# Output product and own embedding of the chosen rows once per two groups, another order of the start, and new lists of steps in a ViT block on one core

## The reference

```python
pooled = x.reshape(64, 12, 14, 16, 14, 16).sum(axis=(3, 5))          # sums of 16x16 patches
h = jnp.einsum('bcij,ce->bije', pooled, channel_weights)              # (64, 196, 192)
y = _layernorm(h)
qkv = y @ Wqkv_w + Wqkv_b                                             # 12 heads of 16
attn = softmax(q @ k^T * 0.25 + causal_mask)                          # mask: -10000 above the diagonal
attn_output = ctx @ out_w + out_b
selection = softmax((y @ sel_w + sel_b) / temperature)[..., 1:]
_, idx = jax.lax.top_k(selection[..., 0], 14)
y = y.at[idx].add((attn_output * selection)[idx])                     # chosen rows alone
h = h + y
h = h + gelu(_layernorm(h) @ in_weight.T + in_bias) @ out_weight      # hidden width 768
```

## Time and profile before

| | |
|---|---|
| median of 3 runs | 708.93 us (699.64 to 709.5) |
| profiled execution | 706.07 us |
| its span, first to last instruction | 704.4 us |
| PE busy | 576.7 us, 82% |
| DVE busy | 522.0 us, 74% |
| ACT busy / POOL busy | 335.0 us / 251.9 us |
| granted PE clock, mean | 0.942 of full speed |

### The profile page before, as it was taken

The page is one execution under the profiler, slowest core; times in us unless marked ns, Lnnn a source line. Parts: engine busy times, 40 slices in busy tenths (PEclk is TensorE's granted clock), DMA queues, the critical chain, the costliest instruction groups (busy, mean ns, idle before and its releaser), DMA issues.

```text
span 704.4 us, 12381 instructions
## 1 busy us (share of the span) xinstructions
PE 576.7 (82%) x3860; PEld 475.4 (67%) x3860; DVE 522.0 (74%) x1103; ACT 335.0 (48%) x826; POOL 251.9 (36%) x484
## 2 busy tenths in 40 slices
PE   0228048899997999889998979799988999899995
PEld 0117027686976787768876777678767887788784
DVE  1767977797979888888887867988888888753411
ACT  0000044565554656554655445465645465547541
POOL 1220433444344525352535323452535253304001
PEclk9998557999999999999998989999999999999998
DMA  9996895989797979887997669797997795001001
GB/s 326 348 363 193 302 350 174 342 276 343 240 336 268 300 253 345 285 302 222 331 302 275 209 232 320 247 309 246 333 302 289 227 331 140 13 10 41 26 9 40
DMA packets 34892, 172.54 MB, mean 245 GB/s; under 512 B 3688, under 2 KB 19240, under 8 KB 22538
## 3 DMA queue, kind: packets, MB, share of 16 engines
q1 hardware_dynamic: 20224, 143.14, 56.0%
q0 software_dynamic: 6912, 11.70, 9.6%
q10 hardware_dynamic: 7690, 16.89, 6.7%
HBM read 158.99 MB, written 12.73 MB: 244 GB/s over the span
## 4 chain that ended last, share of the span: by engine, by line
PE 44%; DVE 18%; issue 16%; POOL 8%; DMA 6%; ACT 5%; POOLq 1%; DVEq 0%; SPq 0%; ACTq 0%
PE psO L637 15%; DMA X<-in_x 6%; PE psS L588 6%; DVE R L942 5%; PE psS L597 4%; PE psF L625 4%; PE psS L576 3%; PE psA L542 2%; DVE mx L1056 2%; PE psS L561 2%; ACT ET L754 2%; POOL b_ln L391 1%; DVE a_ln L952 1%; DVE b_ln L954 1%; DVE y_ln L956 1%
## 5 line engine op out<-in xcount | busy, mean ns | idle before, releaser
L942 DVE TENSOR_REDUCE R<-X 128x42 f32<-128x2688 f32 (+1 forms) x112 | 260.5, 2339 | 15.6 <-POOL X L352 8.5
L637 PE MATMUL psO<-W,act 128*112 128x192 f32 x1344 | 261.8, 339 | 11.9 <-ACT obuf L779 4.0
L637 PEld LDWEIGHTS psO<-W,act 128*112 128x112 f32 x1344 | 223.3, 183 | 18.2 <-issue 7.3
L772 ACT ACTIVATE act<-psF 128x392 f32<-128x392 f32 x192 | 95.3, 496 | 123.1 <-PE psF L625 121.2
L352 POOL TENSOR_TENSOR X<-X 128x1344 f32<-128x1344 f32 x32 | 96.9, 3027 | 21.3 <-DMA X<-in_x 21.1
L361 POOL TENSOR_TENSOR Pt<-Praw 48x196 f32<-48x196 f32 x16 | 8.6, 538 | 191.3 <-DMA Praw<-patch_sums 191.3
L625 PE MATMUL psF<-Stk,M1S 104*128 104x392 bf16 x192 | 66.1, 344 | 5.5 <-ACT act L772 4.8
L1067 DVE TENSOR_TENSOR G<-psS,K 64x336 f32<-64x336 f32 x32 | 16.0, 501 | 44.7 <-PE psS L588 44.2
L588 PE MATMUL psS<-ET,F 98*64 98x336 f32 x128 | 39.6, 452 | 10.4 <-ACT ET L754 10.4
L750 ACT ACTIVATE Sm<-Sm,rinv 112x196 f32<-112x196 f32 x96 | 35.3, 445 | 18.9 <-DVE rinv L1062 18.7
L745 ACT ACTIVATE Sm<-psS,nm 112x196 f32<-112x196 f32 x96 | 39.2, 427 | 7.3 <-DVE nm L1059 7.2
(11 more groups left out here) (197 smaller groups left out, 954.1 us busy)
## 6 DMA issues: line engine op xcount, KB each, us to landing
X<-in_x SPq DMA_DIRECT2D x96, 1344.0 KB, 8.6
X<-in_x SPq DMA_DIRECT2D x16, 672.0 KB, 4.6
X<-in_x POOLq DMA_DIRECT2D x16, 672.0 KB, 12.8
out<-obuf ACTq DMA_DIRECT2D x16, 588.0 KB, 8.7
patch_sums<-R ACTq DMA_DIRECT2D x16, 147.0 KB, 7.9
Praw<-patch_sums ACTq DMA_DIRECT2D x16, 147.0 KB, 6.5
W1T<-in_w1t ACTq DMA_DIRECT2D x1, 576.0 KB
W<-in_w ACTq DMA_DIRECT2D x1, 576.0 KB
```

What stands on the lines that cost most here:

```text
L637: pe.matmul(to, act_sb[u % 2][:, m, i * OT:(i + 1) * OT], W2[:, m, :], start=(m == 0), stop=False)
L772: act.activation(act_sb[u % 2][:, n // 2, (n % 2) * (GT // 2):(n % 2 + 1) * (GT // 2)], psF[:, 0:GT // 2], ACT.Gelu).then_inc(act_F1.sem, 1)
L942: dve.tensor_reduce(R[:, r, t * TQ * N:(t + 1) * TQ * N].rearrange("p (q j) -> p q j", q=TQ), v, AX.XY, ALU.add).then_inc(dve_L, 1)
```

## The change

1. **Chosen rows once per pair.** ZY, G2, dsm, dsel, res and h1 hold both groups of a pair (56 rows, 8 unused, 56 rows). `rs` and `at` are issued for the second group alone and give 120 rows; `rs` goes to psC. G2, ZY and dsel get a memset at the start.
2. **The start.** `prepare` is gone. `first_group` on DVE sums the seven tiles of group 0 between the weight steps and puts the head copies, A4, B2 and the bf16 parts of RS behind the last sum; tiles 0 and 1 of group 1 are summed there too. ACT issues the small selection weights first, W1T once X0 has landed, the attention weights once X2 has, W2 once X5 has.
3. **The lists** of all four engines are new. DVE's `L` steps and `log` move back, PE's `zt` moves ahead and `sl` behind `at:1`, POOL's `c:s` moves behind `H:0`, ACT's exps move from the start of a period to the end of the one before.

```diff
-        ZY = sb("ZY", [FR, SLOTS])
+        ZY = sb("ZY", [FR, 2, ODD])
-        G2 = sb("G2", [128, HP, SLOTS])
-        dsm, dsel = sb("dsm", [SLOTS, GB]), sb("dsel", [SLOTS, 1])
+        G2 = sb("G2", [128, HP, 2, ODD])
+        dsm, dsel = sb("dsm", [PROWS, GB]), sb("dsel", [PROWS, 1])
...
-            plan = ("X:3:1 P:s:2 c:s:5 H:5:1 A:var2:2 K:v:2 K:d1:2 K:d2:2 H:0:0").split()
+            plan = ("P:s:2 H:5:1 A:var2:2 K:v:2 K:d1:2 K:d2:2 H:0:0 c:s:5 X:3:0").split()
...
                     if exists(g - 1):
-                        pe.wait_ge(dve_S.sem, dve_S.at(g - 1, "h1"))
+                        pe.wait_ge(dve_S.sem, dve_S.at(g - 1, "g1"))
+                    if u % 2 == 0 and exists(g - 2):
+                        pe.wait_ge(dve_Q.sem, dve_Q.at(q - 1, "h1"))
...
-                    pe.wait_ge(dve_G.sem, dve_G.at(g, "ix"))
-                    mm = pe.matmul(psS[0:SLOTS, 0, D:2 * D], ZY[:, :], BW[:, :], start=True, stop=True)
...
+            def step_rs(g, q):
+
+                pe.wait_ge(dve_G.sem, dve_G.at(g, "zy"))
+                if exists(g - 2):
+                    pe.wait_ge(dve_C.sem, dve_C.at(q - 1, "os1"))
+                pe.matmul(psC[0:PROWS, 0:D], ZY[:, :, :].rearrange("p e s -> p (e s)")[:, 0:PROWS], BW[:, :],
+                          start=True, stop=True).then_inc(pe_Q.sem, 1)
...
-                mm = pe.matmul(psS[0:SLOTS, 0, 0:D], G2[:, j, :], B2[:, j, :], start=(j == 0), stop=(j == HP - 1))
+                mm = pe.matmul(psS[0:PROWS, 0, 0:D], G2[:, j, :, :].rearrange("p e s -> p (e s)")[:, 0:PROWS], B2[:, j, :],
+                               start=(j == 0), stop=(j == HP - 1))
...
                     elif stage == "at":
-                        step_at(g, 2 * int(step))
-                        step_at(g, 2 * int(step) + 1)
+                        if u % 2:
+                            step_at(g, 2 * int(step))
+                            step_at(g, 2 * int(step) + 1)
...
+                act.dma_start(Wsel[0:DH, :, :], selw.rearrange("(k d) n -> d k n", k=2)).then_inc(w_sel, 16)
...
+                act.wait_ge(x_in[0], loaded(0))
                 act.dma_start(W1T[0:DH, :, :], w1t.rearrange("(k d) n -> d k n", k=2)).then_inc(w_ffn, 16)
...
+                act.wait_ge(x_in[2], loaded(0))
                 act.dma_start(Wqkv[0:DH, :, :], wqkv.rearrange("(k d) n -> d k n", k=2)).then_inc(w_att, 16)
...
+                act.wait_ge(x_in[5], loaded(0))
+                act.dma_start(W2[:, :, :], w2.rearrange("(h p) e -> p h e", h=HT)).then_inc(w_out, 16)
...
-            plan = ("S:e0:2 S:e1:2 S:e2:2 S:e3:2 S:e4:2 S:e5:2 O:0:2 S:n:2 O:1:2 A:fm:1 K:H:1 S:t:2 K:M:1 O:2:2 "
-                    "K:L:1 A:e:1 O:3:2 R:st:0 K:k1:1 K:k2:1 f:0:1 f:1:1 f:2:1 f:3:1 O:4:2 R:ld:0 f:4:1 f:5:1 f:6:1 "
-                    "O:5:2 f:7:1 G:rs:1 C:XH:2 f:8:1 C:ga:2 f:9:1 f:10:1 O:6:2 C:gb:2 f:11:1").split()
+            plan = ("K:H:1 S:t:2 K:M:1 A:fm:1 K:L:1 O:3:2 G:rs:2 R:st:0 K:k1:1 A:e:1 K:k2:1 f:0:1 f:1:1 f:2:1 f:3:1 "
+                    "R:ld:0 f:4:1 O:4:2 f:5:1 f:6:1 O:5:2 f:7:1 f:8:1 C:XH:2 f:9:1 f:10:1 C:ga:2 O:6:2 f:11:1 C:gb:2 "
+                    "S:e0:1 S:e1:1 S:e2:1 S:e3:1 S:e4:1 S:e5:1 O:0:1 S:n:1 O:1:1 O:2:1").split()
...
+            def first_group():
+
+                sum_tile(0, 0, 0)
+                weights_first()
+                sum_tile(0, 0, 1)
+                weights_moments()
+                sum_tile(0, 0, 2)
+                weights_tokens()
+                sum_tile(0, 0, 3)
+                sum_tile(0, 0, 4)
+                weights_ffn()
+                sum_tile(0, 0, 5)
+                weights_parts("M")
+                sum_tile(0, 0, 6)
+                for m in range(3):
+                    weights_heads(m)
+                weights_attention("a4")
+                sum_tile(1, 1, 0)
+                weights_attention("b2")
+                sum_tile(1, 1, 1)
+                weights_parts("R")
+
-            plan = ("C:os:4 S:g:3 A:sel:2 L:0:0 A:top:2 S:at:3 A:slots:2 G:ga:2 C:xh:3 L:1:0 G:u:2 L:2:0 S:sc:2 "
-                    "A:var:1 L:3:0 S:ri:2 L:4:0 A:log:1 L:5:0 L:6:0").split()
+            plan = ("A:log:2 S:g:3 A:sel:2 C:os:4 A:top:2 S:at:3 A:slots:2 G:ga:2 C:xh:3 L:0:0 G:u:2 L:1:0 S:sc:2 "
+                    "A:var:1 L:2:0 S:ri:2 L:3:0 L:4:0 L:5:0 L:6:0").split()
```

More of the change, by code:

```diff
@@ L248, in program @@
         dve_W = Steps(sem("dve_weights"), "wr0 ws0 xh0 h10 as0 ini idb ms ms2 wcs rf mr mr2 wcr bw0 bw1 wt ws cf cf2 raw sd sd2 s1 tp tz tmm tmd tmb m1 "
-                      + " ".join(f"{n}{t}" for t in "MR" for n in splits.split()) + " q k v a4 b2 ob")
+                      + " ".join(f"{n}M" for n in splits.split()) + " q k v a4 b2 ob " + " ".join(f"{n}R" for n in splits.split()))
         block = ctx.enter_context(nc.Block())
@@ L478, in weights @@
                 mm.then_inc(pe_W.sem, 1)
+                pe.wait_ge(w_ffn, NW_FFN * 16)
                 for n in range(2):
@@ L561, in step_G, with step_S @@
                         mm = pe.matmul(psS[0:ZR, 1 + h // HP, (h % HP) * SLOTS:(h % HP + 1) * SLOTS], A4[:, h, :],
[L562 to L566 removed]
+                                       ZY[0:ZR, r, 0:SLOTS], start=True, stop=True)
                 mm.then_inc(pe_G.sem, 1)
[L569 removed]
+            def step_S(g, u, name, q):
                 r = u % 2
@@ L631, in step_F2 @@
                 if m == 0:
+                    if i == 0 and isinstance(g, int) and g == 0:
+                        pe.wait_ge(w_out, 16)
+                        pe.wait_ge(dve_W.sem, dve_W.at(0, "alR"))
                     if i == 0:
@@ L653, in body @@
                         continue
-                    if stage == "C":
+                    if stage == "C" and step == "rs":
+                        if u % 2:
+                            step_rs(g, pair_of(i, k, lag))
+                    elif stage == "C":
                         if u % 2:
@@ L733, in step_R, with step_G @@
                     act.dma_start(Praw[:, r, :], sums_in[bass.ds(g, 1)].rearrange("o p q -> (o p) q")).then_inc(sums_back[r], 16)
-            def step_G(g, u, name):
-                act.wait_ge(pe_G.sem, pe_G.at(g, "rs"))
-                act.activation(res[:, :], psS[0:SLOTS, 0, D:2 * D], ACT.Copy).then_inc(act_G.sem, 1)
+            def step_G(q):
+                act.wait_ge(pe_Q.sem, pe_Q.at(q, "rs"))
+                act.activation(res[:, :], psC[0:PROWS, 0:D], ACT.Copy).then_inc(act_Q.sem, 1)
             def step_S(g, u, name):
@@ L799, in body @@
                         step_F2(g, u, int(step))
+                    elif stage == "G":
+                        if u % 2:
+                            step_G(pair_of(i, k, lag))
                     elif stage == "f":
@@ L1126, in body @@
                     if stage == "L":
-                        if isinstance(i, int) and k == 0:
-                            prepare(int(step))
-                        sum_tile(g, u % 2, int(step))
+                        if not (isinstance(g, int) and (g, int(step)) < (1, 2)):
+                            sum_tile(g, u % 2, int(step))
                     elif stage == "S":
-                        stage_S(g, u, step, pair_of(i, k, lag))
+                        if step != "at" or u % 2:
+                            stage_S(g, u, step, pair_of(i, k, lag))
                     elif stage == "C":
@@ L1136, in body @@
                         {"A": stage_A, "G": stage_G}[stage](g, u, step)
-                if isinstance(i, int) and k == 0:
-                    weights_attention("a4")
-                    weights_attention("b2")
             weights_zeroed()
+            first_group()
             periods(nc.vector, body, 8, 2)
 NW_CW = 1 + PAIRS + 2 * GB + 2
-NW_FFN = 5
-NW_ATT = 5
+NW_SEL = 3
+NW_FFN = 2
+NW_ATT = 4
 def kernel(x, L0_tok_channel_weights, L0_attn_Wqkv_w, L0_attn_Wqkv_b, L0_attn_sel_w, L0_attn_sel_b, L0_attn_out_w,
```

83 lines of the change are left out of this document (36 added, 47 removed), and 3 rows, old and new, of the table plan.

## The result

| | before | changed |
|---|---|---|
| median, first comparison | 707.89 us (699.64 to 709.5) | 719.48 us (711.81 to 733.63) |
| ratio to before | 1 | 1.0172, 95% interval 1.0117 to 1.0227 |
| again, on another chip | 705.96 us | 716.6 us, ratio 1.0166 (1.0129 to 1.0203) |

The changed kernel is 1.7% slower: +12 us where -14 were forecast. Here and in what follows the medians hold every execution, while ratios and intervals leave out the slow ones (over 1.5% above the fastest of their kernel), so where the two differ the ratio counts. Its profile is shown from the execution of the second comparison, 715.07 us with a span of 713.3; the first comparison's profile fell on an execution that took 14 us more than the median.

What follows compares the result with a forecast made beforehand. PE bounds heavy stretches; in light ones POOL's fold holds DVE's nm and PE waits. Terms -8.8 + 2 - 1.5 - 1.2 - 4.5 = -14.0 from 706.07 give 692 us, 8-in-10 range 682 to 706.

Steps and rivals of the forecast that it cites:

- -8.8 - 0.5 - 1.0: Light stretches: 1.7 us less in each of five, 0.3 in a sixth; 0.5 and 1.0 less in the first and last.
- So the work leaves mostly where PE is not the bound: Chosen rows once per pair: at (2.4 us) leaves light stretches, rs (some 0.46 us) leaves heavy ones.
- With a fallen clock in about half of them (1.5 us for twelve records in rows 2) I take 35.4 us.: Light stretch: 34.7 us laid out, 35.4 taken with the clock's fall; bounds 33.3 and 37.
- The fold still meets `nm`: Light stretch: fold runs from 18.9 to 22.0 us behind S:g, nm ready at 20.1, freed 2.8 us earlier than before.
- rival A: Light stretches: the fold ends before nm, the clock holds, 33.6 us, -3.5 each, 683 us in all; chance 0.17.
- Heavy stretches, +0.3 each: Heavy stretches: rs and scores' wait saved, later sl leaves PE dry; +0.3 us each, +2 over seven, bounds -0.5 and +0.9.
- the loop's turn, -1.2: ACT's loop turn moves between O:2 and K:H, ahead of the exps before: -1.2 us, bounds -3 and +1.
- the forecast 42: Sign in the new profile: a window of about 42 us where ACT's loop turns.
- The start, -4.5 us: Start: DVE's sums end at 57.7 instead of 65.74, var starts about 74 instead of 77.83; -4.5 us, bounds -6 and -2.
- no fold runs beside `prod`: Start, DVE: prod runs without a fold beside it, which saves 1.2 us of its 1.48.
- Rival C: Heavy stretches: xh meets tile 5's fold, up to 3.0 us in each of seven, 21 us added, 713 us; chance 0.1.
- Rival D: Chosen rows once per pair: the pairing does nothing, as PE work leaves where PE waits; within the forecast, no separate chance.

Runs made afterwards that it cites:

- lists and start, no pairing: The kernel before with the new lists and the new start, chosen rows still made for every group by itself: 693.98 us, ratio 0.9877.
- POOL's list alone: The kernel before with one line of POOL's list changed, two indirect DMAs moved behind the fold of tile 0: 690.27 us, in more rounds 690.61 us (0.9776).
- changed with filler: The changed kernel with at's six matmuls issued in light stretches too, their result unread, 2.4 us more PE work each: 695.16 us, ratio 0.9887.
- changed with late six: The changed kernel with the same six unread matmuls in light stretches, but behind the scores, right ahead of rs: 714.99 us, ratio 1.0051.
- lists alone: The kernel before with the new lists, old start, rs and at issued for every group: 698.03 us, ratio 0.9898.
- two unread matmuls: The changed kernel with two of at's six matmuls issued unread in light stretches, in the gap ahead of sl: 707.85 us, ratio 1.0035.

## Why the prediction was wrong

Span by parts, in us; light and heavy are the sums of eight and seven windows of the kernel's profile:

| | to first `S:g` | light | heavy | behind the last `S:g` | span |
|---|---|---|---|---|---|
| before | 129.37 | 285.6 | 262.5 | 26.96 | 704.4 |
| changed | 130.11 | 289.8 | 269.9 | 23.48 | 713.3 |
| lists and start, no pairing | 129.50 | 277.0 | 264.0 | 23.66 | 694.1 |
| POOL's list alone | 127.98 | 270.5 | 264.9 | 25.45 | 688.9 |
| changed with filler | 129.28 | 276.7 | 273.4 | 23.53 | 702.9 |
| changed with late six | 128.61 | 296.6 | 261.3 | 23.53 | 710.0 |

The forecast was -14.0 and the execution profiled here came out at +9.0 (715.07 against 706.07): 23.0 us apart. Light stretches are 14.5 of them (forecast -8.8 - 0.5 - 1.0, measured +4.2), heavy ones with the loop's turn 6.6 (+2 - 1.2 against +7.4), the start 5.2 (-4.5 against +0.7), and the end gave 3.5 back.

1. *"So the work leaves mostly where PE is not the bound"*, in the part on chosen rows once per pair. This is the step that failed. It is true that PE isn't the bound there, and the removed 2.4 us were counted as free to take. But those matmuls stood where PE's next steps wait for DVE and ACT, and without them the clock goes to 1.2 GHz for some 10 us in most loaded light stretches. Shown by the filler (20 us back with the work put back unread, and light windows of 276.7 us together, as without the pairing), by its late twin (light windows of 38.3 to 39.0 us with the same work elsewhere) and by the price of the pairing with old and with new lists. The light stretches are 12.8 us of the 19.2 that the profiles of the changed kernel and of the one without the pairing are apart; 5.9 are heavy ones, for which see 4.
2. *"With a fallen clock in about half of them (1.5 us for twelve records in rows 2) I take 35.4 us."* The fall was taken as a consequence of the wait ahead of `zt`. With that wait almost gone it came at another place, in four of the five stretches that the sum counted (and in the sixth), and cost up to 3.7 us instead of 1.5: 38.2 to 38.4 against the 34.7 that I had laid out at full clock. The fifth, behind the loop's turn, has 35.64 us with a fall at its start. The layout itself held: with `at` put back, or with lists alone, and the clock at 1.00, loaded light windows are 34.0 to 35.0 us.
3. *The fold still meets `nm`.* The fold came at 18.84 as laid out, but even at full clock the scores start at 18.0 (filler) or 18.3 (lists alone) and not at 16.5, so `nm` is ready at about 22.0, when the fold ends. I had PE's path to the scores 1.5 us too short. In the changed kernel and with lists alone the collision went entirely (`nm` 0.17 us everywhere), as in rival A; with the filler it takes 0.27 to 1.40 us in four stretches. Worth of it by POOL's list alone: 285.6 - 270.5 = 15.1 us over the light stretches, near the 17.5 of rival A's -3.5 in each of five. Rival A was right in that the collision goes, though in the changed kernel partly because the slow matmuls make `nm` late; its clock didn't hold, since the same change took `at` out.
4. *Heavy stretches, +0.3 each, and the loop's turn, -1.2.* Five of the seven windows add 0.5 us together. One is 39.16 us at a clock of 0.91 where 36.67 stood, and the one of the loop's turn is 47.69 instead of 43.26. ACT still stands idle there, 5.11 us instead of 5.93, as its timeline shows:

```profile
434.11 0.73 ACT L735 ACTIVATE SP<-v 98x624 bf16<-98x624 f32 x1 [5.11 <-issue]
```

The kernels with two unread matmuls or six late ones, with the same lists and the pairing, have 41.49 and 41.68 us in this window, near the forecast 42. Most of the 6 more here is a second stop of PE in the middle of an output tile, for which the profile shows no wait:

```profile
427.36 1.12 PE L651 MATMUL psO<-W,act 128*112 128x192 f32 x3 [4.79 <-issue]
```

In it the clock falls to the half level, for 6.8 us. The first profile of the changed kernel has the same second stop (4.46 us), and no other kernel has it; the kernel with the late six stops there once, for 0.79 us. What makes PE stop stays open.
5. *The start, -4.5 us.* It gained nothing: ratio 1.0033 alone, and 0.9821 against 0.9776 on top of POOL's list, within both intervals. The layout was right up to the last sum: it began at 54.55 and ended at 57.50 (forecast 57.7, 65.74), and POOL had P at 69.86 instead of 76.64. But `var` started at 78.43, not at 74 (rows of DVE in the changed kernel):

```profile
68.18 1.36 DVE L929 COPY B<-psS 128x1152 f32<-128x1152 f32 x1 [3.73 <-PE psS L508]
69.58 3.46 DVE L932 SCALAR_TENSOR_TENSOR B<-OB,K,B 64x192 f32<-64x192 f32 x1
72.97 2.94 DVE L972 TENSOR_REDUCE R<-X 128x42 f32<-128x2688 f32 x1
78.43 0.38 DVE L998 COPY F<-psA 98x216 f32<-98x216 f32 x1
```

and of PE and POOL beside them:

```profile
61.78 6.36 PE L508 MATMUL psS<-act,obuf 16*64 16x192 f32 x24
73.09 1.03 PE L519 MATMUL psA<-TMR,P 49*98 49x108 f32 x4 [4.95 <-DVE B L932]
```

```profile
69.82 3.00 POOL L356 TENSOR_TENSOR X<-X 128x1344 f32<-128x1344 f32 x1
```

Two terms were missed. PE's product for B2 takes 6.36 us, not the 4.4 that I read off the kernel before, since the clock is at the half from 62 us on. And the fold, which comes earlier together with P, now holds the addition to B (3.46 us, until the fold's end at 72.82), on which `tm` waits: I wrote that no fold runs beside `prod`, and didn't ask beside what it would run. The 6.8 us by which P came earlier were all spent waiting for DVE, and the first `S:g` stands at 130.11 instead of 129.37. In the last 40 us ahead of it PE's clock is lower than before the change, 0.58 instead of 0.69.
6. *Rival C, `xh` meets the fold.* Not in the profile above: `xh` takes 0.38 us at 405.53, and PE waits 0.40 us for it. It does occur, now and then: twice in the changed kernel's first profile (`xh` held for 3.59 and 3.52 us, in windows of 42.46 and 44.89 us), and once in the filler's profile, where DVE and POOL stood so:

```profile
477.66 3.70 DVE L1119 TENSOR_SCALAR xh<-h,mv,y_lnC 120x192 f32<-120x192 f32 x1
```

```profile
478.24 3.00 POOL L356 TENSOR_TENSOR X<-X 128x1344 f32<-128x1344 f32 x1
```

PE waited 4.51 us ahead of `xt`, and that heavy window is 42.95 us. All three stand in executions 9 to 14 us above their kernel's median. The mechanism holds, the "each of seven heavy stretches" doesn't.
7. *Rival D, "the pairing does nothing"*, was counted into the forecast without a price on the other side. Its true price, +20 us, is larger than all the gains of the sum (16 us).

The Trainium skill, "TensorE: Matmul & The Clock Gate", section "Why this matters for your kernels", names long idle gaps between bursts of matmuls as what brings the clock down. The trace shows the clock fall behind four gaps of which the longest is 1.33 us, so a reader who only looks for long gaps by that section would have passed this stretch, as I did.

## What to carry to other kernels

Work that stands in an engine's waits isn't always free to remove: on PE, look at what the granted clock does in the stretch that it leaves, and price the stretch at the half level too (here 34.3 or 38.4 us). Before a large rewrite, try its smallest part alone: one line of POOL's list gave 2%, and the rest of the change took it away and 12 us more. A collision that is moved away from one victim has to be followed to its next neighbour (`nm` freed, B's addition and now and then `xh` caught).
